# Attention of the experts as one written-out pipeline over all heads; turning and input products ride in the next block

## The reference

```python
qkv = h @ aiw + aib
q, k, v = jnp.split(qkv, 3, axis=-1)
q, k, v = (heads(q), heads(k), heads(v))
attn = jax.nn.softmax(jnp.einsum('bhqd,bhkd->bhqk', q, k) * SCALE, axis=-1)
o = jnp.einsum('bhqk,bhkd->bhqd', attn, v).transpose(0, 2, 1, 3).reshape(h.shape)
h = o @ aow + aob
hf = _lstm_dir(h, wif, whf, bf)                    # inside: zg = xt @ Wi + h @ Wh + b
hb = _lstm_dir(h[:, ::-1], wibk, whbk, bbk)[:, ::-1]
```

## Time and profile before

| | |
|---|---|
| profiled execution | 5917.21 us, its span 5915.4 us |
| PE, DVE, ACT, POOL busy over the span | 91%, 75%, 39%, 16% |
| encoder's end to the first matmul of `experts_attend` | 763 to 782 us |
| `experts_attend`, first matmul to the first instruction of the next stage | 782.3 to 2475 us |
| `recurrence` (L1318 and others) | about 2475 to 5400 us |
| mean granted TensorE clock | 0.963 of 2.4 GHz |

### The profile page before, as it was taken

The page is one execution under the profiler, slowest core; times in us unless marked ns, Lnnn a source line. Parts: engine busy times, 40 slices in busy tenths (PEclk is TensorE's granted clock), DMA queues, the critical chain, the costliest instruction groups (busy, mean ns, idle before and its releaser), DMA issues. The chain is left out here.

```text
span 5915.4 us, 261478 instructions
## 1 busy us (share of the span) xinstructions
PE 5379.3 (91%) x108704; PEld 3590.6 (61%) x108704; DVE 4411.6 (75%) x20301; ACT 2334.2 (39%) x8423; POOL 944.5 (16%) x4109
## 2 busy tenths in 40 slices
PE   7878879989889998699999999999999999998895
PEld 4545523323323333288888888888888888884442
DVE  4546567666676676699999999999999999993224
ACT  2334444444354354433333333333333333333332
POOL 0000000000000000033333333333333333330000
PEclk9989989989989999899999999999999999999997
DMA  0003353334343334401111011111011111002110
GB/s 12 0 20 119 112 105 79 73 82 86 86 78 84 93 58 82 153 15 36 26 31 36 20 30 36 28 29 36 21 29 36 23 34 36 16 19 79 58 43 11
DMA packets 378664, 302.83 MB, mean 51 GB/s; under 512 B 146074, under 2 KB 358682, under 8 KB 373563
## 3 DMA queue, kind: packets, MB, share of 16 engines
q1 hardware_dynamic: 378510, 301.15, 21.4%
HBM read 182.09 MB, written 120.59 MB: 51 GB/s over the span
## 5 line engine op out<-in xcount | busy, mean ns | idle before, releaser
L1318 PE MATMUL bank<-lparts,lstate 128*32 128x256 bf16 x98304 | 2784.8, 273 | 103.2 <-DVE lstate L1364 55.5
L1318 PEld LDWEIGHTS bank<-lparts,lstate 128*32 128x32 bf16 x98304 | 2459.1, 97 | 429.4 <-DVE lstate L1364 252.4
L1395 ACT ACTIVATE ltc<-lgc 128x16 f32<-128x16 f32 x2049 | 442.6, 216 | 1763.8 <-DVE lgc L1350 1763.5
L1329 DVE STREAM_TRANSPOSE ltz<-bank 128x256 f32<-128x256 f32 x2048 | 920.8, 450 | 98.3 <-PE bank L1318 19.9
L1051 DVE TENSOR_REDUCE bnegmax<-bank 128x1 f32<-128x512 f32 x1024 | 650.1, 679 | 257.0 <-PE bank L981 255.7
L1411 POOL TENSOR_TENSOR wh<-lgate,ltc 128x16 f32<-128x16 f32 x2052 | 465.6, 227 | 1936.7 <-ACT ltc L1395 1862.5
L1096 ACT ACTIVATE wh<-bank 128x512 f32<-128x512 f32 x1024 | 554.9, 598 | 296.9 <-PE bank L1003 290.0
L1418 POOL COPY ltz<-wh 128x64 f32<-128x64 f32 x2048 | 605.8, 296 | 0.0
L883 PE MATMUL bank<-xT,bw 128*128 128x512 f32 x1024 | 537.0, 626 | 56.6 <-DVE bzs L894 50.2
L1336 DVE TENSOR_TENSOR lhalf<-ltz 128x128 f32<-128x128 f32 x2048 | 576.8, 282 | 12.1 <-POOL ltz L1418 11.4
L1346 DVE TENSOR_TENSOR lprod<-lgate,lgc 128x32 f32<-128x32 f32 x2049 | 472.7, 231 | 46.2 <-ACT lgc L1391 46.2
(11 more groups left out here) (211 smaller groups left out, 4848.0 us busy)
## 6 DMA issues: line engine op xcount, KB each, us to landing
zx<-bzs SPq DMA_DIRECT2D x32, 2048.0 KB, 6.8
wh<-zx SPq DMA_DIRECT2D x64, 1024.0 KB, 7.4
bqp<-qk SPq DMA_DIRECT2D x198, 128.0 KB, 4.7
bkp<-qk SPq DMA_DIRECT2D x198, 128.0 KB, 7.9
qk<-eparts SPq DMA_DIRECT2D x96, 256.0 KB, 2.6
hs<-wh SPq DMA_DIRECT2D x32, 512.0 KB, 5.8
cmemT<-hs SPq DMA_DIRECT2D x32, 512.0 KB, 4.3
bw<-in_w_attend SPq DMA_DIRECT2D x4, 2304.0 KB, 11.5
```

What stands on the lines that cost most here:

```text
L1318: last = nc.tensor.matmul(bank[x][32 * q:32 * q + 32, 0:256], top[:, x, e, k].rearrange("p m r -> p (m r)"), parts[:, way, g, k, n, e, q], ...
L1329: nc.vector.transpose(tz[:, x].rearrange("p (n w) -> p n w", w=SLOT)[:, :, 0:32], bank[x][:, 0:256].rearrange("p (n c) -> p n c", n=BLOCKS ...
L1395: nc.scalar.activation(tc[:, x], gc[:, x, 1], ACT.Tanh).then_inc(tanhed[x], 1)
```

## The change

All 16 blocks become one program without a loop or a barrier: 256 head steps, numbered j, and a few more at the end. Semaphores count on from block to block and are not cleared in between.

- In step j the heads' work stands as before, but `score_t(j - 2, 3)` now comes ahead of `turn_maxima(j - 1)`, and `keep_rows` behind the fourth exponential.
- A block is turned in the five steps 6 to 10 after its heads (`at` 0 to 4), piece by piece, all in bank 7. Its 16 products follow in the next eleven steps, one and two in turn; a product's two matmuls now stand together. The 16th product of a block ends one step ahead of the next block's turning. This holds for blocks 0 to 14; the last one is turned at the end as before, its products in four banks.
- The stretch behind the fourth block of an expert, the barriers and the separate first blocks are gone: the first block of an expert has the turning and products of the expert before beside it. The weights are loaded in three pieces, each when its last use is over. `vx` has two buffers.
- The copy inside DRAM and the barrier before the first block are gone.
- `zs` and `zx` are laid out by 16 time steps, then gate block, then time: `keep_product` writes runs of 16 floats, and POOL's copy in the recurrence finds the gate blocks 16 floats apart, where they were adjacent. The DMAs move the same bytes.

The core of the diff (the old functions are printed above; the tail of the last block, the loads and `split`, `exponent`, `values`, `divide`, `keep_rows` differ only in their counts, or in two buffers for `vx`):

```diff
...
-        zs = core.sb(ctx, "bzs", [P, 2, S, BLOCKS])
...
+        zs = core.sb(ctx, "bzs", [P, 2, S // ZX_STEPS, BLOCKS, ZX_STEPS])
...
+        TURN_AT, PRODUCTS_AT = 6, 11
...
+        LAST_STEP = HEADS + 6
+        LATE_BANKS = (7, 5, 0, 1)
...
+        def products_of(j):
+            at = (j - PRODUCTS_AT) % NH
+            slab = (j - PRODUCTS_AT) // NH - 1
+            if slab < 0 or at >= len(PRODUCTS_IN_STEP):
+                return slab, 0, 0
+            first = sum(PRODUCTS_IN_STEP[:at])
+            return slab, first, first + PRODUCTS_IN_STEP[at]
...
+        def turned_in(j):
+            slab = (j - TURN_AT) // NH - 1
+            return (slab, (j - TURN_AT) % NH) if 0 <= slab < SLABS - 1 else (slab, -1)
+        def product_bank(slab, n):
+            return bank[LATE_BANKS[n % len(LATE_BANKS)] if slab == SLABS - 1 else 7]
...
+                    if slab < SLABS - 1:
+                        if slab > 0:
+                            sp.wait_ge(valued, NH * slab)
+                        load_values(slab + 1)
+                        sp.wait_ge(scored_t, BT * NH * slab + BT * NH // 2)
...
+                def turn_values(slab, qt):
+                    if qt == 0:
+                        pe.wait_ge(o_kept, 4 * (slab + 1))
+                        if slab > 0:
+                            pe.wait_ge(z_kept, NH * slab)
+                    elif slab < SLABS - 1:
+                        pe.wait_ge(on_done, BT * slab + qt)
+                    for g in range(4):
...
+                    if k > 0 and slab < SLABS - 1:
+                        pe.wait_ge(oT_kept, KH * slab + k)
...
+                    elif slab < SLABS - 1:
+                        pe.wait_ge(a_kept, KH * slab + m)
...
+                        held = len(LATE_BANKS) if slab == SLABS - 1 else 1
+                        if n == 0:
+                            pe.wait_ge(a_kept, KH * (slab + 1))
+                        elif n >= held:
+                            pe.wait_ge(z_kept, NH * slab + n - held + 1)
+                        if block == 0 and slab % B == 0:
...
+                pe.wait_ge(zeroed, 3)
+                for j in range(LAST_STEP):
+                    slab, at = turned_in(j)
+                    made, first, end = products_of(j)
+                    if j < HEADS:
+                        score(j, 0)
+                        score(j, 1)
+                    if 2 <= j < HEADS + 2:
+                        for kt in range(3):
+                            score_t(j - 2, kt)
+                    if at == 1:
+                        turn_values(slab, 1)
+                    elif at == 2:
+                        turn_values(slab, 3)
+                    elif at == 3:
+                        turn_divided(slab, 0)
+                    elif at == 4:
+                        project(slab, 0)
+                    elif end > first:
+                        for k in range(KH):
+                            product(made, first, k)
+                    if j < HEADS:
+                        score(j, 2)
+                        score(j, 3)
+                    if 2 <= j < HEADS + 2:
+                        score_t(j - 2, 3)
+                    if at == 0:
+                        turn_values(slab, 0)
+                    elif at == 1:
+                        turn_values(slab, 2)
+                    elif at == 3:
+                        turn_divided(slab, 1)
+                    elif at == 4:
+                        project(slab, 1)
+                    elif end > first + 1:
+                        for k in range(KH):
+                            product(made, end - 1, k)
+                    if 1 <= j < HEADS + 1:
+                        turn_maxima(j - 1)
+                    if j >= 6:
+                        values((j - 6) // 4, (j - 6) % 4)
+                for qt in range(BT):
+                    turn_values(SLABS - 1, qt)
...
+                def keep_product(slab, n):
+                    way, block = divmod(n, BLOCKS)
...
+                        dve.wait_ge(z_stored[way], 16 * slab)
+                    nc.vector.tensor_scalar(zs[:, way, :, block],
+                                            product_bank(slab, n)[:].rearrange("p (c t) -> p c t", t=ZX_STEPS),
+                                            cols[:, COLS["lb"] + n:COLS["lb"] + n + 1], None, ALU.add).then_inc(z_kept, 1)
...
+                    slab, at = turned_in(j)
+                    earlier, first_before, end_before = products_of(j - 1)
+                    made, first, end = products_of(j)
+                    if end_before > first_before + 1:
+                        keep_product(earlier, end_before - 1)
+                    if at == 1:
+                        divide(slab, 0)
+                    elif at == 2:
+                        divide(slab, 2)
+                    if j < HEADS:
+                        largest(j, 0)
+                        largest(j, 1)
+                    if end > first:
+                        keep_product(made, first)
+                    if at == 1:
+                        divide(slab, 1)
+                    elif at == 2:
...
+                                         bias=cols[:, COLS["aob"] + m:COLS["aob"] + m + 1]).then_inc(a_kept, 1)
+                for j in range(LAST_STEP):
+                    slab, at = turned_in(j)
+                    if j >= 10 and j % 4 == 2:
+                        keep_values((j - 10) // 4)
+                    if at == 4:
+                        keep_divided(slab, 1)
+                    elif at == 5:
+                        keep_projected(slab, 1)
+                    if 2 <= j < HEADS + 2:
+                        for kt in range(3):
+                            exponent(j - 2, kt)
+                    if at == 3:
+                        keep_divided(slab, 0)
+                    elif at == 4:
+                        keep_projected(slab, 0)
+                    if 2 <= j < HEADS + 2:
+                        exponent(j - 2, 3)
...
-            "p (w f g t n) -> p w f g t n", w=2, f=2, g=E * B, t=ZX_STEPS)
+            "p (w f g n t) -> p w f g n t", w=2, f=2, g=E * B, t=ZX_STEPS)
...
-                    nc.gpsimd.tensor_copy(rows, zx[:, way, i // ZX_STEPS % 2, 8 * g:8 * g + 8, at].rearrange(
+                    nc.gpsimd.tensor_copy(rows, zx[:, way, i // ZX_STEPS % 2, 8 * g:8 * g + 8, :, at].rearrange(
...
```

More of the change, by code:

```diff
@@ L872, in experts_attend @@
-        HEADS_IN = 2 * len(PAIRS) * 16
-        def product(pe, n, k, banks):
-            way, block = divmod(n, BLOCKS)
-            if k == 0:
-                if n == 0:
-                    pe.wait_ge(a_kept, KH)
-                elif n >= len(banks):
-                    pe.wait_ge(z_kept, n - len(banks) + 1)
-            at = ATT["wi"] + (way * KH + k) * G4 + block * P
-            last = nc.tensor.matmul(bank[banks[n % len(banks)]][:], w[:, at:at + P], aT[:, k], start=k == 0,
-                                    stop=k == KH - 1)
-            if k == KH - 1:
-                last.then_inc(z_mm, 1)
@@ L937, in project @@
-        def project(pe):
-            pe.wait_ge(oT_kept, KH)
-            for m in range(KH):
-                for k in range(KH):
-                    at = ATT["aow"] + k * DM + m * P
-                    last = nc.tensor.matmul(project_banks[m][:], w[:, at:at + P], oT[:, k], start=k == 0,
-                                            stop=k == KH - 1)
-                last.then_inc(a_mm, 1)
-        def keep_projected(act):
-            for m in range(KH):
-                act.wait_ge(a_mm, m + 1)
-                nc.scalar.activation(aT[:, m], project_banks[m][:], ACT.Identity,
-                                     bias=cols[:, COLS["aob"] + m:COLS["aob"] + m + 1]).then_inc(a_kept, 1)
@@ L1124, in _, with load_heads @@
             def _(sp):
-                sp.dma_start(d["qk"][E * B], d["qk"][0]).then_inc(filled, 16)
-                load_heads(sp, 0, 0)
-                sp.wait_ge(qk_in[0], HEADS_IN)
-                sp.wait_ge(filled, 16)
+                def load_heads(slab, half):
+                    heads = slice(half * NH // 2, (half + 1) * NH // 2)
+                    for side, dst in ((0, qp), (1, kp)):
+                        for n, pair in enumerate(PAIRS):
+                            src = d["qk"][slab, side, pair[side]].rearrange("(h r) n -> r h n", r=DH)
+                            sp.dma_start(dst[n * DH:(n + 1) * DH, heads], src[:, heads]).then_inc(qk_in[half], 16)
@@ new lines, in _ @@
+                nc.vector.memset(kp[KROWS:KROWS + 3], 1.0).then_inc(zeroed, 1)
+                nc.vector.tensor_copy(ident16[:], core.ident[:]).then_inc(zeroed, 1)
+                nc.vector.memset(bank[6][:], 0.0).then_inc(zeroed, 1)
+                for j in range(LAST_STEP + 1):
+                    slab, at = turned_in(j)
[15 more added lines that the diff above has]
+                    elif at == 2:
+                        divide(slab, 3)
+                    if j < HEADS:
```

(4 more changed lines are left out.)

453 lines of the change are left out of this document (209 added, 244 removed).

## The result

The changed kernel takes 5648.5 us (median of 4 runs, 5647.1 to 5650.0) against 5913.9 us for the kernel before on the same chip (5910.6 to 5916.0): a ratio of 0.9552, 95% interval 0.9535 to 0.9568.

What follows compares the result with a forecast made beforehand. PE bounds blocks with products, PE and DVE first blocks; stretches without heads idle the heads' engines. Start 856.9, fifteen periods of 92.0, end and tail give 2274.5, 200.5 us earlier: 5716.7, forecast 5720 us; range 5675 to 5805.

Steps and rivals of the forecast that it cites:

- The eviction: keep_product, 1142 ns before, was to take 0.75 us with the new layout; bounds 0.69 and 1.14.
- rival 1: Eviction stays at 1.14 us since the gap between runs sets it: 61 us in 15 periods, 5781 us; chance 10%.
- The first score: Start of the stage: without DRAM copy and barrier, between 0 and 12 us earlier, 6 taken, so 776.3.
- The steps up to the turning: From the first score to step 22, the later steps at 3.71 us each: 80.6 us, ending at 856.9.
- The five turning steps: Steps in which a block is turned through bank 7: 25 us together; bounds 24 (nothing waits) and 30.
- The stage's tail: From the end of the last values to the next stage: 49.9 us less a barrier of 2.3, so 47.6.
- The recurrence: POOL's copy, 293 ns in the median, keeps its time under the new address pattern; bounds 0 and twice the time.
- rival 4: Slower than before: POOL's copy lengthens in the recurrence; at twice the time 6190 us; chance 5%, 4 of them slower.
- Fresh code: Code without a loop: 0.9 us a block at most, 13 us in all, or 0 if streamed ahead.
- Rival 2: Chains through bank 7 hold PE like the block boundaries did: period 100.8, 132 us more, 5852 us; chance 14%.
- Rival 3: The counted waits don't come and PE runs at its own work: period 87 us, 5645 us; chance 5%.
- the price of a step with one product: Steady head step, 5.47 us before: terms sum to 5.22, taken as 5.15 us for the new order.

Runs made afterwards that it cites:

- a_layout: The changed kernel with only the old layout of zs and zx, so keep_product writes floats 32 bytes apart again: 5711.8 us, ratio 0.9656.
- a_late2: The changed kernel with the second product of a step moved behind the values, to the end of the step: 5623.4 us, ratio 0.9508.
- b_layout: The kernel before with only the new layout of zs and zx: 5838.6 us, ratio 0.9877.
- a_order: The changed kernel with the maxima turned ahead of the fourth transposed score again, as before: 5651.7 us, ratio 0.9555.
- b_order: The kernel before with only the new order: fourth transposed score, then maxima, then values: 5880.3 us, ratio 0.9951.
- b_all2: The kernel before with new order, new layout, joined product halves, and each product evicted in its own step between second and third maximum: 5828.1 us, ratio 0.9853.

## Why the prediction was off

**Right.** The eviction: 0.75 us said, 751 ns measured, and a_layout gives rival 1 its price. The first score: its distance from SP's first load fell by 5.0 us (19.1 to 14.1), 6 said. The steps up to the turning: 78.7 us (780.50 to 859.21), 80.6 said, but with two errors that partly cancel: the fifteen steps were 0.23 us shorter each, and the seven before them 1.4 us longer in all. The five turning steps: 24.4 in the period (23.9 the first time), 25 said, 24 the bound below. The stage's tail: 47.0, 47.6 said. The recurrence: POOL's copy 294 ns against 296 in the means, and 294 to 297 ns in every kernel of either layout, so rival 4 falls. From first to last matmul the recurrence was 2840.2 us and is 2833.4; over all kernels here it lies between 2831 and 2840 with either layout. Fresh code costs nothing that shows: PE is busy for 56.0 of 57 us in the window of the steady part, which lies in the first pass.

**Rival 2** falls: no chain through bank 7 holds PE as long as the block boundaries did. **Rival 3** gave 5645 us and a period of 87, and both came; but its reason, that the waits don't come, is only half true. The second product of a step does wait: a_late2 gains 25 us by giving it more to hide behind, and the bracket understates the wait. By the measured terms PE's own work in a period is 16 x (4.73 - 1.71) + 16 x 1.71 + 6.6 = 82 us, and the other 5 to 6 us are waits. So rival 3's 87 had work too dear and waits at nothing; that its time came is luck.

**The step that failed is "the price of a step with one product"**, and with it that with two. The forecast had 5.15 and 7.22, the trace has 4.73 and 6.98. Per period 6 x 0.42 + 5 x 0.24 = 3.7 us, and 0.6 from turning; the distance of the turnings gives 92.0 - 87.67 = 4.3, times 15 that is 65 of the 71 us. Another 3 us are the allowance for code between the sum of 5716.7 and the forecast of 5720. The terms that were mis-sized:
- *"three transposed scores 0.96 less the wait of 0.15, so 0.81"*: it is 0.65 (883.53 to 884.18, and in b_layout), so 0.16 too much. I subtracted the idle bracket. A matmul's end is modelled in the record, and an idle time inside that tail isn't shown. The distance between starts, beside the same three without a wait, gives 0.31.
- *"a whole product is 0.96 + 0.86 = 1.82"*: it is 1.71 behind the transposed scores and 1.82 (892.68 to 894.50 in a_late2) behind the values. I took the 0.96 from the half that stood behind a wait; 0.11 too much. The rows below have a half that waited for nothing, 0.86.
- *"1.17 for two scores, the maxima and the fourth transposed score; the values 0.98"*, 2.15 less 0.07 for the order: it is 1.92 (885.89 to 887.81). Scores and fourth transposed score take 0.75 in one row (885.89 to 886.64), where it was 1.17 less the 0.32 of the maxima (893.07 to 893.39 in a_order), 0.85; and maxima and values 1.17, not 0.32 + 0.98. Together 0.23, which is also what b_order and a_order measure for the order by itself; I had allowed 0.07.

0.16 + 0.11 + 0.16 = 0.43, the whole of it. The second term, and nearly half of the first, would have followed from the trace of before, from the first step with a product of a block, where bank 7 is free:

```profile
1066.58 0.90 PE L1003 MATMUL bank<-bqp,bkp 99*128 99x512 bf16 x3
1067.32 1.02 PE L883 MATMUL bank<-xT,bw 128*128 128x512 f32 x2
1068.18 0.59 PE L981 MATMUL bank<-bkp,bqp 96*128 96x512 bf16 x2
```

Three transposed scores take 0.74 us here and half a product 0.86. The third term couldn't be read there, since no maxima stand directly ahead of values in that kernel.

The second product of a step was priced too low, which hides in the 7.22: it costs 6.98 - 4.73 = 2.25 us, and 1.82 + 0.25 = 2.07 was said. The 1.01 us from the end of one product to the start of the next came as forecast (890.69 to 891.70), but the work in between is 0.44 + 0.22 = 0.66 us and not 0.76, so the wait is 0.35; and the product takes 1.91 (891.70 to 893.61).

**Where the 265 us come from.** Layout, order, joining and the place of the eviction, all in the old structure, give 87 us (b_all2). The remaining 179 or so belong to the one pipeline over the blocks, which the experiments show only as this difference. The traces say where they lie. From turning to turning there are twelve distances inside an expert, 94.4 us in the mean in b_all2; in the changed kernel they are 87.67, and 78.2 for the last one, since the last block is turned as soon as its heads are done. That makes 90 us. The three distances that span two experts are 120.0, 116.6 and 112.1 us in b_all2, so 86 more. Together these are 176 us; the last turning comes 46 us ahead of the next stage in both. The part of the recurrence that ran shorter has no cause in the change that shows here.

Some of the 176 us are the clock, which no run separates. In the kernel before, behind the stretch without heads and 10.6 us of idle PE, the next expert's first block starts at the lower level, 1.2 GHz (same columns as above):

```profile
1203.50:1232.00 28.50, 27.13 (x80) 7.56 (x80) 22.23 (x56) 14.39 (x26) 0.00 (x0) 0.50 0.60 121
```

A step without values takes 4.04 us there (1213.98 to 1218.02) and 3.20 at a granted clock of 1.00 (799.77 to 802.97). The first blocks of the second to fourth expert take 73.3 to 73.9 us, that of the first 70.1; by that, an estimate, the low clock behind the three stretches costs about 11 us. Over the stage the granted clock was 0.95 before (0.95 in b_all2 too) and is 0.99.

The effects don't add: layout alone gives 72, order alone 31, joining -31, the three together 45. With the loop through DVE in charge (5.06 us) what PE saves inside a step is lost. When the eviction leaves that loop (b_all2), the step falls to 4.80. That the joining pays isn't shown even then: layout and order without it weren't run together, and their single gains, 72 + 31, come to more than the 87 of b_all2.

## What to carry to other kernels

Price an operation by the distance between starts in a stretch without a wait, not by a distance less an idle bracket: on PE the bracket showed 0.15 of 0.31 us, and in two kernels nothing of 0.2. When work is joined or moved, follow the loop around it once through every engine, and count what each engine has queued in front: here the place of one 0.75 us eviction, ahead of or behind two maxima and a 0.7 us split, was worth 38 us. And put a product that waits for a bank behind the longest piece of other work in its step; that gave the last 25 us.

## What the runs showed of the hardware

- DVE writes 512 floats a partition from PSUM in 1140 to 1149 ns when each stands 32 bytes from the next, and in 750 to 751 when they stand in runs of 16, though the runs lie 512 bytes apart: the gap between runs costs nothing that shows. The same 751 as for a contiguous output.
- Maxima (bf16, three output partitions) and the first values (f32) behind them start 0.01 us apart on PE and take 1.17 us together, where apart they take 0.32 and 0.98 (a_order). With head 3's values first, which share the maxima's output partitions, they start 0.12 us apart, and the total is the same.
- POOL's copy takes 294 to 297 ns whether the gate blocks lie 4 or 64 bytes apart.
- Straight code showed no fetch stall: PE stood for under 1 us in a window of 57 us of code that ran for the first time.
- A step without a product or values took 4.04 us at a granted clock of 0.50 (1.2 GHz) and 3.20 at 1.00 (2.4 GHz), in the trace of before at 1214 and 800 us.
